# The attention output projection and its layer norms, moved from a stage of their own into the feed-forward chunks

## What is computed

```python
def _L0_attn_ref(x, Wq, Wk, Wv, Wo, bo, Wconv):
    kc = conv(x, Wconv, stride=3)                 # keys from a strided convolution
    k_tmp = concatenate([x[:, :1, :], kc], axis=1)  # 1,366 key positions
    q, k, v = x @ Wq.T, k_tmp @ Wk.T, k_tmp @ Wv.T
    p = softmax(q k^T / 8 + mask)
    return (p v) @ Wo.T + bo

def _L0_ffn_ref(x, ...):
    h = silu(x @ w1.T * w1_s) * (x @ w2.T * w2_s)
    h = gelu(h @ h1.T * h1_s)
    h = gelu(h @ h2.T * h2_s)
    return h @ w3.T * w3_s

x = x + layernorm(_L0_attn_ref(layernorm(x), ...))
x = x + layernorm(_L0_ffn_ref(layernorm(x), ...))
```

## Time and profile before

| What | us |
|---|---|
| Timed executions, two | 6817.63 and 6766.89, median 6792.26 |
| The profiled execution | 6439.48 |
| Span of its slowest core, core 1 | 6437.7 |
| Span of its fastest core, core 4 | 6344.3 |

### The profile page before, as it was taken

One profiled execution on the slowest core, in us unless ns is written; L12 is line 12 of the kernel. 1 busy time (PEld: TensorE's weight loads), 2 busy tenths in 40 slices (PEclk: granted clock), 3 DMA queues, 4 the chain that ended last, 5 costly groups with the idle time before them and its releaser, 6 DMA issues.

```text
span 6437.7 us, 38984 instructions; the slowest of 8 cores (6344.3 to 6437.7 us)
## 1 busy us (share of the span) xinstructions
PE 3299.0 (51%) x15168; PEld 1468.5 (23%) x15168; DVE 706.7 (11%) x1430; ACT 598.0 (9%) x880; POOL 98.2 (2%) x192
## 2 busy tenths in 40 slices
PE   0000255534444000201124998599966999669994
PEld 0000012212222000100011443244422334224441
DVE  0044201122211000340000000100002000020001
ACT  0000000022332000100000000110001000011000
...
GB/s 127 143 97 98 90 72 66 47 101 179 125 119 187 129 195 122 84 74 199 199 143 122 152 139 117 104 150 144 145 96 126 124 118 144 97 119 144 144 144 78
DMA packets 1378644, 804.82 MB, mean 125 GB/s; under 512 B 607248, under 2 KB 1338528, under 8 KB 1364128
## 3 DMA queue, kind: packets, MB, share of 16 engines
...
## 4 chain that ended last, share of the span: by engine, by line
PE 44%; DMA 28%; another core or an unknown queue 12%; SPq 8%; DVE 4%; issue 4%; ACT 0%; POOL 0%; DVEq 0%; POOLq 0%; ACTq 0%
PE ps_f L1163 29%; DMA p2b<-n_h 6%; PE ps_f L1101 5%; DMA t_h<-p2b 4%; PE ps_f L1224 4%; DMA wbuf<-t_w 3%; DMA p2b<-n_w 3%; PE ps_cv L462 3%; DMA t_w<-p2b 2%; DVE ln_st L311 2%; SPq L877 2%; DMA lx<-x_full 2%; DMA cv_nat<-wconv 2%; SPq L450 1%
## 5 line engine op out<-in xcount | busy, mean ns | idle before, releaser
L1163 PE MATMUL ps_f<-hslab,wbuf 128*128 128x512 bf16 x4096 | 940.1, 396 | 42.1 <-DMA wbuf<-t_h 42.1
L1163 PE MATMUL ps_f<-cslab,wbuf 128*128 128x512 bf16 x4096 | 901.5, 384 | 41.6 <-DMA wbuf<-t_h 41.6
L1101 PE MATMUL ps_f<-x2fm,wbuf 128*128 128x512 bf16 x2048 | 489.3, 404 | 772.9 <-DMA wbuf<-t_w 771.6
L462 PE MATMUL ps_cv<-xwin,wt_cv 128*128 128x512 bf16 (+1 forms) x576 | 183.1, 483 | 896.4 <-DMA wt_cv<-n_cv 896.4
L1163 PEld LDWEIGHTS ps_f<-hslab,wbuf 128*128 128x128 bf16 x4096 | 413.4, 101 | 568.9 <-issue 210.8
L1163 PEld LDWEIGHTS ps_f<-cslab,wbuf 128*128 128x128 bf16 x4096 | 404.4, 99 | 538.8 <-issue 82.3
L1101 PEld LDWEIGHTS ps_f<-x2fm,wbuf 128*128 128x128 bf16 x2048 | 208.4, 103 | 1053.7 <-issue 845.9
L971 PE MATMUL ps_w<-ofm,wt_o 128*128 128x512 bf16 x256 | 64.4, 417 | 606.5 <-DMA ofm<-scr_o 602.9
L1224 PE MATMUL ps_f<-hslab,wbuf 128*128 128x512 bf16 x1024 | 260.5, 422 | 207.9 <-DMA wbuf<-t_w 207.9
L462 PEld LDWEIGHTS ps_cv<-xwin,wt_cv 128*128 128x128 bf16 x576 | 59.8, 105 | 1019.3 <-issue 1002.0
L311 DVE TENSOR_REDUCE ln_st<-ff_tm 128x1 f32<-128x1024 bf16 x16 | 19.5, 1217 | 2438.3 <-DMA ff_tm<-scr_ff 2438.3
...
## 6 DMA issues: line engine op xcount, KB each, us to landing
wbuf<-t_h SPq DMA_DIRECT2D x256, 1024.0 KB, 9.4
...
t_h<-p2b POOLq DMA_DIRECT2D x64, 1024.0 KB, 4.2
wbuf<-t_w SPq DMA_DIRECT2D x128, 512.0 KB, 5.5
wbuf<-t_w SPq DMA_DIRECT2D x32, 1024.0 KB, 8.0
n_w<-w POOLq DMA_DIRECT2D x16, 1024.0 KB, 162.5
...
t_w<-p2b POOLq DMA_DIRECT2D x16, 1024.0 KB, 4.2
```

The source lines that it names most:

```text
L462: ins = t.matmul(ps_cv[ot][:, 0:pn], wt_cv_t(kd)[:, ot * 128:(ot + 1) * 128], xwin_t(kd)[:, w:3 * (pn - 1) + w + 1:3], start=(w == 0 and k ...
L1101: ins = t.matmul(ps[:, 0:TC], wbuf_t(par, 8 * w12 + kd)[:, mt * 128:(mt + 1) * 128], x2fm_t(kd), start=(kd == 0), stop=(kd == DT - 1))
L1163: ins = t.matmul(pb[mt][:, 0:TC], wbuf_t(par, k)[:, mt * 128:(mt + 1) * 128], src_t(k), start=(k == 0), stop=(k == DHT - 1))
```

## The change

The a3 stage goes. Its tiles move into the feed-forward part. Its group 0 is listed ahead of chunk 0. Groups 1 to 3 are cut into bundles, and one bundle of group C+1 is listed after each block of chunk C (`pump(1)`). The list of a group is: 1 bundle that loads `ofm`, 6 empty ones, the 8 blocks of the Wo product with bias and store, 2 empty ones, and 12 with the two layer norms of the group's 4 tiles. So the `ofm` load stands behind block 0 of the up-projection, the 8 Wo blocks stand behind its blocks 7 to 14, and the 12 layer norm bundles stand behind blocks 1 to 12 of the first hidden-layer pass.

To make room, xp is not kept: each tile is stored to the new DRAM tensor `scr_xp`, and LN4 loads it back into `xpl`, a buffer of two tiles. `ofm` and the temporaries have one buffer where they had two. The up-projection uses 4 PSUM banks and not 8, and hands over each 128 columns (m) by themselves; banks 4 and 5 belong to the Wo product. The stores of `otm` stand behind each pair of attention tiles in SP's queue, and not behind all of them. The preparation steps keep their places. LN4 is listed in another order.

```diff
+                def _so(sy, jp=jp, val=cnt["cV"]):
+                    wait(sy, "cV", val)
+                    for j in (2 * jp, 2 * jp + 1):
+                        inc(sy.dma_start(scr_o[j * 128:(j + 1) * 128, :], otm_t(j)), "dSO")
+                bb.sync(_so)
             emit_p2(len(p2_steps))
             ev["otm"] = cnt["cV"]
+            ev["scr_o"] = cnt["dSO"]
+            ev["attn_T"] = cnt["cT"]
+            ev["attn_A"] = cnt["cA"]
...
-            def _ow(sy):
-                wait(sy, "cV", ev["otm"])
-                for j in range(NJ):
-                    inc(sy.dma_start(scr_o[j * 128:(j + 1) * 128, :], otm_t(j)), "dSO")
-                ev["scr_o"] = cnt["dSO"]
-                wait(sy, "dgA", ev["dgA"])
-                for kd in range(DT):
-                    inc(sy.dma_start(wt_o_t(kd), n_wo[:, kd * 128:(kd + 1) * 128],
-                                     transpose=True), "dWK")
-                ev["woT"] = cnt["dWK"]
-            bb.sync(_ow)
...
-            for grp in range(NJ // 4):
...
-                if grp >= 1:
-                    for jj in range(4):
-                        j = (grp - 1) * 4 + jj
-                        a3_front(j)
-                        if j >= 2:
-                            a3_finish(j - 2)
-                            ln2_front(j - 2)
-                        if j >= 4:
-                            ln2_finish(j - 4)
...
+            ln_tmp = fb.enter_context(nc.sbuf_tensor("ln_tmp", [128, D], F32, side="right"))
...
+            ofm = fb.enter_context(nc.sbuf_tensor("ofm", [128, DT * 512], BF16, side="right"))
...
+            xpg = fb.enter_context(nc.sbuf_tensor("xpg", [128, 4 * D], F32, side="right"))
+            xpl = fb.enter_context(nc.sbuf_tensor("xpl", [128, 2 * D], F32, side="right"))
...
+            ps_w = [ps_f[4], ps_f[5]]
...
+            def a3_ofl(g):
+                def _ofl(sy, g=g):
+                    if g == 0:
+                        wait(sy, "cV", ev["consts"])
+                        wait(sy, "cT", ev["attn_T"])
+                    wait(sy, "cT", ev.get(f"wo_mm_g{g - 1}", 0))
+                    wait(sy, "dSO", ev["scr_o"])
+                    for kd in range(DT):
+                        inc(sy.dma_start(ofm_t(kd),
+                                         scr_o[g * 512:(g + 1) * 512, kd * 128:(kd + 1) * 128],
+                                         transpose=True), "dOF0")
+                    ev[f"ofl{g}"] = cnt["dOF0"]
+                bb.sync(_ofl)
+
+            def a3_wo_m(g, m):
+                def _mm(t, g=g, m=m):
+                    if g == 0 and m == 0:
+                        wait(t, "cV", ev["otm"])
+                        wait(t, "cA", ev["attn_A"])
+                    wait(t, "dOF0", ev[f"ofl{g}"])
+                    wait(t, "dWK", ev["woT"])
+                    wait(t, "cA", ev.get(f"at_ev{m % 2}", 0))
+                    for kd in range(DT):
+                        ins = t.matmul(ps_w[m % 2][:, 0:512],
+                                       wt_o_t(kd)[:, m * 128:(m + 1) * 128],
+                                       ofm_t(kd),
+                                       start=(kd == 0), stop=(kd == DT - 1))
+                    ev["at_mm"] = inc(ins, "cT")
+                    if m == DT - 1:
+                        ev[f"wo_mm_g{g}"] = ev["at_mm"]
...
+                def _st(sy, g=g, m=m):
+                    wait(sy, "cA", ev["at_act"])
+                    ev[f"at_w{m % 2}"] = inc(sy.dma_start(
+                        scr_at[m * 128:(m + 1) * 128, g * 512:(g + 1) * 512],
+                        at_sb[:, (m % 2) * 512:(m % 2) * 512 + 512]), f"dAT{m % 2}")
+                    if m == DT - 1:
+                        ev[f"at_grp{g}"] = (cnt["dAT0"], cnt["dAT1"])
+                bb.sync(_st)
...
+            def a3_front(j):
+                slot = j % 4
+                g = j // 4
+
+                def _l(sy, j=j, slot=slot, g=g):
+                    wait(sy, "dAT0", ev[f"at_grp{g}"][0])
+                    wait(sy, "dAT1", ev[f"at_grp{g}"][1])
+                    wait(sy, "cV", ev.get(f"lb2{j - 4}", 0))
+                    wait(sy, f"dXP{j % 4}", ev.get(f"xpw{j - 4}", 0))
+                    inc(sy.dma_start(at_tm[:, slot * D:(slot + 1) * D],
+                                     scr_at[:, j * 128:(j + 1) * 128], transpose=True),
+                        f"dTM{slot}")
+                    ev[f"resx{j}"] = inc(sy.dma_start(xpg_t(j), x_own[j * 128:(j + 1) * 128, :]),
+                                         f"dTM{slot}")
+                bb.sync(_l)
...
+            def a3_finish(j):
+                slot = j % 4
+                c0 = 4 * slot
+
+                def _f(v, j=j, slot=slot, c0=c0, vprev=cnt["cV"]):
+                    wait(v, "cA", ev[f"a3rstd{j}"])
+                    wait(v, f"dTM{slot}", ev[f"resx{j}"])
+                    wait(v, "cV", vprev)
+                    inc(v.tensor_scalar(ln_tmp[:, :], at_tm[:, slot * D:(slot + 1) * D],
+                                        ln_st[:, c0:c0 + 1], ln_st[:, c0 + 2:c0 + 3],
+                                        op0=ALU.add, op1=ALU.mult), "cV")
+                    wait(v, "cV", cnt["cV"])
+                    ins = v.tensor_tensor(xpg_t(j), xpg_t(j), ln_tmp[:, :], ALU.add)
+                    ev[f"xp{j}"] = inc(ins, "cV")
+                bb.vector(_f)
+
+                def _sp(sy, j=j):
+                    wait(sy, "cV", ev[f"xp{j}"])
+                    ev[f"xpw{j}"] = inc(sy.dma_start(scr_xp[j * 128:(j + 1) * 128, :],
+                                                     xpg_t(j)), f"dXP{j % 4}")
...
+                                          op0=ALU.add, op1=ALU.mult)
+                    ev[f"lb2{j}"] = inc(ins, "cV")
+                bb.vector(_f)
+
+                def _w(sy, j=j, b2=b2):
+                    wait(sy, "cV", ev[f"lb2{j}"])
...
+            def pump(n):
+                while n > 0 and a3_pend:
+                    f_ = a3_pend.pop(0)
+                    if f_ is not None:
+                        f_()
+                    n -= 1
+
+            def a3_group_bundles(g):
+                js = [4 * g + i_ for i_ in range(4)]
+                out = []
+                if g == 0:
+                    out.append(woT_load)
+                out.append(lambda g=g: a3_ofl(g))
+                out.extend([None] * 6)
+                for m in range(DT):
+                    out.append(lambda g=g, m=m: a3_wo_m(g, m))
+                out.extend([None] * 2)
+                out.append(lambda j=js[0]: a3_front(j))
+                out.append(lambda j=js[1]: a3_front(j))
+                out.append(lambda j=js[0]: (a3_finish(j), ln2_front(j)))
+                out.append(lambda j=js[2]: a3_front(j))
+                out.append(lambda j=js[1]: (a3_finish(j), ln2_front(j)))
+                out.append(lambda j=js[3]: a3_front(j))
+                out.append(lambda j=js[2]: (a3_finish(j), ln2_front(j)))
+                out.append(lambda j=js[0]: ln2_finish(j))
+                out.append(lambda j=js[3]: (a3_finish(j), ln2_front(j)))
+                out.append(lambda j=js[1]: ln2_finish(j))
+                out.append(lambda j=js[2]: ln2_finish(j))
+                out.append(lambda j=js[3]: ln2_finish(j))
+                return out
+
+            for f_ in a3_group_bundles(0):
+                if f_ is not None:
+                    f_()
+
             for C in range(NCH):
+                pump(10 ** 6)
+                if C + 1 < NCH:
+                    a3_pend.extend(a3_group_bundles(C + 1))
+
                 def _x2l(sy, C=C):
-                    for s_ in range(2):
-                        wait(sy, f"dX2S{s_}", ev[f"x2w{14 + s_}"])
+                    wait(sy, "dX2S0", ev[f"x2w{4 * C + 2}"])
+                    wait(sy, "dX2S1", ev[f"x2w{4 * C + 3}"])
                     if C > 0:
                         wait(sy, "cT", ev.get(f"ab_mm_all{C - 1}", 0))
                     for kd in range(DT):
@@ -1067,16 +1084,15 @@
                 prev_T_ab = cnt["cT"]
                 for mb in range(DH // 256):
                     par = mb % 2
-                    pb = ps_f[4 * par:4 * par + 4]
...
-                    def _wl(sy, mb=mb, par=par, C=C):
+                    def _wl(sy, mb=mb, par=par, C=C, prev_T_ab=prev_T_ab):
...
-                    def _mm(t, mb=mb, par=par, pb=pb):
-                        wait(t, f"dW{par}", ev[f"wl_ab{mb}"])
-                        wait(t, "dX2", ev["x2fm"])
-                        wait(t, "cV", ev.get(f"h_ev{mb - 2}", 0))
-                        for w12 in range(2):
-                            for mt in range(2):
-                                ps = pb[w12 * 2 + mt]
-                                for kd in range(DT):
-                                    ins = t.matmul(ps[:, 0:TC],
-                                                   wbuf_t(par, 8 * w12 + kd)[:, mt * 128:(mt + 1) * 128],
-                                                   x2fm_t(kd),
```

(48 more changed lines are left out.)

218 lines of the change are left out of this document (79 added, 139 removed), and 2 rows, old and new, of the table sems.

## The result

| What | us |
|---|---|
| After, 36 executions | median 6537.26, 6451.05 to 6843.39 |
| Before, 35 executions | median 6482.07, 6376.62 to 6822.93 |
| Ratio after / before | 1.0123, 95% interval 1.0088 to 1.0157 |
| The profiled execution after, slowest core | 6463.09, span 6461.4 (core 3) |

The change costs 1.2%, within the 2% of "same" and clearly not zero. The two executions of before that were shown ahead of the prediction, 6767 and 6818, stand near the upper end of the 35: some executions of either kernel run several per cent longer at a lower clock, and the two medians of the table hold them while the ratio leaves them out. A forecast of 6841 that is built on the median of those two could not meet a median of 6537, however good its terms.

The account below looks back on a forecast made before the run. Bound: waits outside TensorE (44% of the span), in a3 and chunk 0's weight preparation; TensorE in chunk 1's up-projection. -243 + 98 + 181 + 13 = +49 us, carried onto 6792: 6841 us, chance 0.76; range 6700 to 6960.

Parts of the forecast that it names:

- same: Whole kernel: the change stays within 2% (136 us) of the time before; chance 0.75.
- first rival: Up-projections: Wo stores don't hold SP up, so weight loads stay covered; -198 us, 6594 us; chance 0.07.
- Term 1: a3 stage: shrinks to group 0, so `x2fm` is loaded at 2640 us, not 2883; -243 us.
- The stores at no cost: SP's queue ahead of the Wo load: moving the scr_o (`otm`) stores among the preparation steps costs nothing.
- Term 2: Chunk 0's up-projection: Wo stores delay eight preparation steps by 11.7 us each, the `ofm` load adds 4; +98 us.
- Term 3: Chunks 1 and 2's up-projections: Wo stores take the weight loads' cover, 11.3 us for each of 8 blocks; +181 us.
- Term 4: LN4: loads of the third and fourth tile wait for earlier results on SP, about 3 us per chunk; +13 us.
- Term 5: Hidden-layer passes: the bundles and the smaller PSUM share cost nothing; 0 us, bounds 0 and 30.

Follow-up runs that it names:

- defer2: The changed kernel with the stores of groups 1 to 3's Wo blocks listed two weight loads later in SP's queue; ratio 0.9708 to the kernel before.
- earlystore: The kernel before with only the otm stores listed behind each pair of attention tiles, as in the changed kernel; ratio 0.9994.
- nocover: The kernel before with weight loads of blocks 8 to 15 in chunks 1 and 2's up-projection waiting for block mb-1, not mb-2; ratio 1.0169 on second timing.
- wohidden: The changed kernel with each group's bundles 16 blocks later, Wo blocks in the first hidden-layer pass; no ratio, shortest execution 6543.2 us, 1.023 times before's.

## Why the prediction was right and wrong

- **The level was wrong.** The step that failed is "so I carry the difference over: 6841". It took two executions for the typical ones, although the profiled execution, 5.5% below, contradicted them. The range of 6700 to 6960 was laid around that level and left 6537 out. 35 executions have a median of 6482. On that the forecast +49 is 6531, against 6537 measured, but that this comes within 6 us is luck: the ratio puts the change at about 80 us, not at the 55 between these two medians. The prediction said that the runs lay above the profile and then gave the profile no weight. By the number alone, the first rival's 6594 came closer than the forecast, though its mechanism is not there.
- **Term 1, the shorter a3: -243 forecast, -258 measured.** From the first `ofm` transpose to the `x2fm` load it is 83.6 us, where it was 2883.1 - 2554.5 = 328.6: -245, right within 2 us. The other 13 are ahead of the stage, and the working has no term for them. 3 of them lie between the last casts and the `ofm` load; the rest lies ahead of the casts. It goes with the execution as much as with the kernel: the `ofm` load starts between 2540 and 2566 us on the cores before and between 2526 and 2546 after, but between 2571 and 2606 in defer2, which has the same program up to there.
- **The stores at no cost: right.** Shown by earlystore.
- **Term 2, chunk 0: +98 forecast, +107 measured.** The block shown costs 12.1 us, and the eight together 93.6, 11.7 each as in the working. The `ofm` load behind block 0 costs 6.8 where 4 was forecast: the next preparation step starts 16.1 us after the block's first load, before 9.3. Some 6 us are spread over the rest.
- **Term 3, chunks 1 and 2: +181 forecast, +204 measured.** The mechanism is shown three times: taken away by defer2, made alone by nocover, moved to another place by wohidden. The size was short by 11 us a chunk. A gap is 8.4 us on average in chunk 1 and 8.0 in chunk 2, not 7.5 (the parts of the working add up to 7.6), which only the shortest ones come near (7.74, with a load that lands in 5.9). The clock takes 2.2 us a block and not 2.0 (147.5 us busy, less 114 and 14, less the 1.7 behind the `ofm` gap, over 8). And the `ofm` load behind block 0 costs chunks 1 and 2 a gap of 2.7 and 4.7 us, which the working counted in chunk 0 only. The 2.0 was read between a gap of 3.0 us that cost nothing and one of 10.6; that the price lies between them by the gap's length is not borne out, as the gap of 2.73 us has the same slow matmuls behind it as those of 8.
- **Term 4, LN4: +13 forecast.** The gaps grew by 6.3, 9.2 and 5.4 us where 3 was forecast, and chunk 3 with its LN4 by 7.8. The working had the right waits at too small a price: VectorE stands idle for 4.44 and 4.49 us ahead of the third and the fourth tile (the rows of LN4 above).
- **Term 5, the hidden layers: 0 forecast, -2.9 measured.** Right, in chunks 0 and 1. Twelve bundles in a pass cost nothing there: all that TensorE waits for loads in the four first passes is 44.4 us, which is the wait of 10.6 to 12.4 us at the head of each.
- **The sum: +49 forecast, +76 in the profiles.** Same sign, and short by a third: terms 2, 3 and 4 by 9, 23 and 16, against 15 that term 1 brought more and 4 by which chunk 3's up-projection and the hidden layers came out shorter. As a share, +0.8% lies just below the interval of the ratio, +0.9 to +1.6%. "Same" had 0.75, and it came. The first rival, that the loads stay covered, described what defer2 is, not what the change is: -198 forecast for it, and its ratio of 0.971 is -188 on the 6439.5 of the profiled execution.
